# Six of seven layer-0 parts in high and low halves, a turn by 39 columns, and sum and halves placed sooner in a DLRM tower kernel

## The reference

```python
e = stack of the 39 gathered rows                        # (512, 39, 16)
x0 = xk = e
for W in (f0, f1, f2):                                   # (39*39, 128), (128*39, 128), (128*39, 128)
    z = einsum('bfd,bgd->bfgd', x0, xk).reshape(b, f * g, d)
    xk = einsum('bpd,pm->bmd', z, W)
    outs.append(xk)
h = concat(sum(concat(outs, 1), -1), dense_ctx)          # (512, 384 + 16)
y = relu(relu(h @ W1 + b1) @ W2 + b2) @ W3
```

## Time and profile before

| | |
|---|---|
| runs | 699.26 us median of 3 (698.6 to 702.59) |
| profiled execution | 700.51 us, span of its instructions 698.7 us |
| granted TensorE clock | 0.985 over the span, 1.00 in the loop |
| busy | PE 643.2, DVE 538.7, ACT 518.5, POOL 429.9 us |

### The profile page before, as it was taken

The page is one execution under the profiler, slowest core; times in us unless marked ns, Lnnn a source line. Parts: engine busy times, 40 slices in busy tenths (PEclk is TensorE's granted clock), DMA queues, the critical chain, the costliest instruction groups (busy, mean ns, idle before and its releaser), DMA issues. The chain is left out here.

```text
span 698.7 us, 11739 instructions
## 1 busy us (share of the span) xinstructions
PE 643.2 (92%) x2567; PEld 472.3 (68%) x2567; DVE 538.7 (77%) x1216; ACT 518.5 (74%) x1842; POOL 429.9 (62%) x416
## 2 busy tenths in 40 slices
PE   0578999999999999999999999999999999999988
PEld 0246777676767677777777676767676777776663
DVE  1426788888887979797988888888979797999880
ACT  1226688788797878787887888787878787888862
POOL 6876568686767676767678686767676534101330
PEclk9877999999999999999999999999999999999999
DMA  7551332231304040313131221313040320301000
GB/s 206 117 118 30 88 74 45 45 72 37 80 10 106 9 107 3 85 31 77 39 77 40 56 61 39 77 23 93 9 108 4 96 63 0 109 0 44 29 1 0
DMA packets 58221, 40.28 MB, mean 58 GB/s; under 512 B 36626, under 2 KB 41056, under 8 KB 58203
## 3 DMA queue, kind: packets, MB, share of 16 engines
q1 hardware_dynamic: 52376, 38.73, 22.1%
q0 software_dynamic: 5120, 1.29, 2.4%
q10 hardware_dynamic: 706, 0.06, 0.1%
HBM read 38.13 MB, written 1.94 MB: 57 GB/s over the span
## 5 line engine op out<-in xcount | busy, mean ns | idle before, releaser
L640 ACT ACTIVATE parts<-psa,x0c 128x128 f32<-128x128 f32 x1536 | 440.7, 431 | 94.6 <-PE psa L793 88.2
L532 DVE SCALAR_TENSOR_TENSOR parts<-psd,x0c,parts 128x128 f32<-128x128 f32 x960 | 266.0, 342 | 80.9 <-PE psd L793 64.1
L503 DVE TENSOR_REDUCE cur<-parts 128x64 f32<-128x1536 f32 x128 | 223.6, 1747 | 23.7 <-ACT parts L640 18.8
L789 PE MATMUL psa<-w1h,x1h 128*128 128x512 f32 x384 | 175.3, 457 | 5.9 <-issue 5.9
L793 PE MATMUL psa<-w1h,x1l 128*128 128x512 f32 x384 | 152.4, 397 | 0.0
L790 PE MATMUL psa<-w1l,x1h 128*128 128x512 f32 x384 | 152.2, 396 | 0.0
L359 POOL TENSOR_TENSOR z0l<-pairs,z0h 117x512 fp32r<-117x512 f32 x56 | 72.7, 1298 | 122.6 <-ACT z0h L596 122.4
L343 POOL DMA_INDIRECT emb<-tables,idx x130 | 126.7, 975 | 23.3 <-issue 19.8
L352 POOL TENSOR_TENSOR pairs<-x0t,pairs 117x512 f32<-117x512 f32 (+1 forms) x105 | 135.1, 1296 | 7.3 <-DMA x0t<-x_rows 6.6
L789 PE MATMUL psd<-w1h,x1h 128*128 128x512 f32 (+1 forms) x256 | 115.2, 450 | 12.1 <-DVE parts L532 12.1
L793 PE MATMUL psd<-w1h,x1l 128*128 128x512 f32 (+1 forms) x256 | 97.8, 382 | 0.0
(11 more groups left out here) (83 smaller groups left out, 524.5 us busy)
## 6 DMA issues: line engine op xcount, KB each, us to landing
pairs<-x_rows SPq DMA_DIRECT2D x113, 156.0 KB
pairs<-x_rows SPq DMA_DIRECT2D x30, 234.0 KB
x0t<-x_rows SPq DMA_DIRECT2D x16, 234.0 KB
emb<-tables,idx POOLq DMA_INDIRECT x130
x_rows<-emb SPq DMA_DIRECT2D x13, 72.0 KB
wt_sb<-w_top SPq DMA_DIRECT2D x1, 768.0 KB, 5.9
parts<-w SPq DMA_DIRECT2D x1, 704.0 KB, 4.9
x_rows<-emb SPq DMA_DIRECT2D x13, 40.0 KB
```

The source lines that it names most:

```text
L503: return dve.tensor_reduce(cur1[:, t % 2, first:end], terms[:, first:end, :, :], AX.XY, ALU.add)
L532: op = dve.scalar_tensor_tensor(acc, y[:, M * j:M * j + M], x0c[:, t, GF * g + j:GF * g + j + 1], acc, ALU.mult, ALU.add)
L640: op = act.activation(lanes(dst, j), y[:, M * j:M * j + M], ACT.Copy, scale=x0c[:, t, GF * g + j:GF * g + j + 1])
L789: pe.matmul(y[:, 0:n], hi, w1h[:, c], start=True, stop=False)
```

## The change

- `SPLIT` has parts 0 to 5; part 6 stays plain and is now the last one. The halves lie in rings, five buffers for high and four for low ones, so a sixth high half waits for part 0 of the same block, the fifth and sixth low half for parts 0 and 1.
- The three early halves of block b + 2 are made behind ACT (2,4), (3,2) and (3,4) (before: part 2 alone, at (3,4)); POOL subtracts 0 and 1 ahead of its last gather, 2 behind it.
- Parts 0, 1 and 2 of layer 0 go one group sooner, part 6 from (1,5) to (1,9), the turn from (0,8) to (0,9).
- The turn is a plain matmul of 39 rows and 39 columns instead of a transpose of 117.
- Sum over d: DVE (2,2) to (2,0). High halves of x1: ACT (2,4), (3,0), (3,2) to (2,1), (2,3), (3,0). Low halves: DVE (2,3), (3,0), (3,1) to (2,1), (2,2), (3,1). Block 0 keeps its own places for these.

```diff
-L0_AT = {(0, 5): 0, (0, 7): 1, (0, 9): 2, (1, 1): 3, (1, 3): 4, (1, 5): 6, (1, 8): 5}
-L0_AT_FIRST = {(1, 6): 0, (1, 8): 1, (2, 0): 2, (2, 2): 3, (2, 4): 4, (2, 6): 6, (2, 8): 5}
-TURN_AT, TURN_AT_FIRST = (0, 8), (1, 5)
+L0_AT = {(0, 4): [0], (0, 6): [1], (0, 8): [2], (1, 1): [3], (1, 3): [4], (1, 8): [5], (1, 9): [6]}
+L0_AT_FIRST = {(1, 6): [0], (1, 8): [1], (2, 0): [2], (2, 2): [3], (2, 4): [4], (2, 6): [5], (2, 8): [6]}
+TURN_AT, TURN_AT_FIRST = (0, 9), (1, 5)
-SPLIT = [2, 3, 4, 5]
-L0_END = 5
+SPLIT = [0, 1, 2, 3, 4, 5]
+L0_END = 6
+HIGHS, LOWS = 5, 4
-ZH_EARLY_AT = {(3, 4): 2}
+ZH_EARLY_AT = {(2, 4): 0, (3, 2): 1, (3, 4): 2}
-SUM_AT, SUM_AT_FIRST = (2, 2), (3, 0)
-HIGH_AT = {(2, 4): 0, (3, 0): 1, (3, 2): 2}
+SUM_AT, SUM_AT_FIRST = (2, 0), (3, 0)
+HIGH_AT = {(2, 1): 0, (2, 3): 1, (3, 0): 2}
-LOW_AT = {(2, 3): 0, (3, 0): 1, (3, 1): 2}
+LOW_AT = {(2, 1): 0, (2, 2): 1, (3, 1): 2}
...
+        def high_slot(i):
+            return z0h[0:ROWS, COLS * (i % HIGHS):COLS * (i % HIGHS) + COLS]
+
+        def low_slot(i):
+            return z0l[0:ROWS, COLS * (i % LOWS):COLS * (i % LOWS) + COLS]
...
                 pool.wait_ge(z0h_ready, (b - 2) * NS + i + 1)
+                pool.wait_ge(l0_steps, L0T * b + (SPLIT[i - LOWS] + 1 if i >= LOWS else 0))
...
                 if gather_ahead:
                     gather(8)
                 if ahead2:
+                    pair_low_part(b + 2, 0)
+                    pair_low_part(b + 2, 1)
+                if gather_ahead:
+                    gather(9)
+                if ahead2:
                     pair_low_part(b + 2, 2)
-                if gather_ahead:
-                    gather(9)
...
                 act.wait_ge(z0_ready, (b - 1) * L0T + k + 1)
-                act.wait_ge(l0_steps, L0T * b)
+                act.wait_ge(l0_steps, L0T * b + (SPLIT[i - HIGHS] + 1 if i >= HIGHS else 0))
...
-                act.activation(x0c[:, t, 0:F], pst[:, ROWS * t:ROWS * t + F], ACT.Copy).then_inc(x0c_ready, 1)
+                act.activation(x0c[:, t, 0:F], pst[:, F * t:F * t + F], ACT.Copy).then_inc(x0c_ready, 1)
...
-                    op = pe.transpose(pst[:, ROWS * t:ROWS * t + ROWS], x0t[0:ROWS, 128 * t:128 * t + 128], ident_sb[0:ROWS, :])
+                    op = pe.matmul(pst[:, F * t:F * t + F], x0t[0:F, 128 * t:128 * t + 128], ident_sb[0:F, :], start=True, stop=True)
```

More of the change, by code:

```diff
@@ L137, in build @@
         mask_sb = sb("mask_sb", [128, TB])
-        ident_sb = sb("ident_sb", [128, ROWS])
+        ident_sb = sb("ident_sb", [128, F])
         ids_sb = sb("ids_sb", [128, (NBLK + 1) * CH], I32)
@@ L148, in build @@
         pairs = sb("pairs", [128, L0T, COLS])
-        z0h = sb("z0h", [128, NS * COLS], F32R)
-        z0l = sb("z0l", [128, NS * COLS], F32R)
+        z0h = sb("z0h", [128, HIGHS * COLS], F32R)
+        z0l = sb("z0l", [128, LOWS * COLS], F32R)
         x1h = sb("x1h", [128, COLS], F32R)
@@ L357, in pair_low_part @@
                 pool.wait_ge(z0h_ready, (b - 2) * NS + i + 1)
-                c = slice(COLS * i, COLS * i + COLS)
-                pool.tensor_tensor(z0l[0:ROWS, c], pairs[0:ROWS, k, :], z0h[0:ROWS, c].bitcast(F32),
+                pool.wait_ge(l0_steps, L0T * b + (SPLIT[i - LOWS] + 1 if i >= LOWS else 0))
+                pool.tensor_tensor(low_slot(i), pairs[0:ROWS, k, :], high_slot(i).bitcast(F32),
                                    ALU.subtract).then_inc(z0l_ready, 1)
@@ L390, in first_block @@
                 gather_early(0, 9)
+                pair_low_part(2, 0)
+                pair_low_part(2, 1)
                 pair_low_part(2, 2)
@@ L438, in block_of @@
                 if ahead2:
-                    pair_low_part(b + 2, 2)
+                    pair_low_part(b + 2, 0)
+                    pair_low_part(b + 2, 1)
                 if gather_ahead:
                     gather(9)
+                if ahead2:
+                    pair_low_part(b + 2, 2)
             pool.wait_ge(ids_in, 16)
@@ L593, in pair_high_part @@
                 act.wait_ge(z0_ready, (b - 1) * L0T + k + 1)
-                act.wait_ge(l0_steps, L0T * b)
-                c = slice(COLS * i, COLS * i + COLS)
-                act.activation(z0h[0:ROWS, c], pairs[0:ROWS, k, :], ACT.Copy).then_inc(z0h_ready, 1)
+                act.wait_ge(l0_steps, L0T * b + (SPLIT[i - HIGHS] + 1 if i >= HIGHS else 0))
+                act.activation(high_slot(i), pairs[0:ROWS, k, :], ACT.Copy).then_inc(z0h_ready, 1)
             def high_part(b, t):
@@ L660, in block_of @@
                                 scalars(b + 1, SCALARS_AT[t, n])
-            act.dma_start(ident_sb[0:ROWS, :], ident).then_inc(const_in, 16)
+            act.dma_start(ident_sb[0:F, :], ident).then_inc(const_in, 16)
             act.dma_start(mask_sb[:, :], mask).then_inc(const_in, 16)
@@ L739, in layer0 @@
                     pe.wait_ge(z0l_ready, (b - 2) * NS + i + 1)
-                    c = slice(COLS * i, COLS * i + COLS)
                     w = slice(M * i, M * i + M)
-                    pe.matmul(ps0[:, :], w0h[0:ROWS, w], z0h[0:ROWS, c], start=False, stop=False)
-                    pe.matmul(ps0[:, :], w0h[0:ROWS, w], z0l[0:ROWS, c], start=False, stop=False)
-                    pe.matmul(ps0[:, :], w0l[0:ROWS, w], z0h[0:ROWS, c], start=False, stop=(k == L0_END)).then_inc(l0_steps, 1)
+                    pe.matmul(ps0[:, :], w0h[0:ROWS, w], high_slot(i), start=(k == 0), stop=False)
+                    pe.matmul(ps0[:, :], w0h[0:ROWS, w], low_slot(i), start=False, stop=False)
+                    pe.matmul(ps0[:, :], w0l[0:ROWS, w], high_slot(i), start=False, stop=(k == L0_END)).then_inc(l0_steps, 1)
                     return
@@ L795, in block_of @@
                             l0_at = L0_AT_FIRST if starts(b) else L0_AT
-                            if (t, g) in l0_at:
-                                layer0(b + 1, l0_at[t, g])
+                            for k in l0_at.get((t, g), []):
+                                layer0(b + 1, k)
                             if (t, g) == (TURN_AT_FIRST if starts(b) else TURN_AT):
@@ L809, in _ @@
             turn_x0(0)
-            for k in [*(k for k in range(L0T) if k != L0_END), L0_END]:
+            for k in range(L0T):
                 layer0(0, k)
@@ L918 @@
         "sample_mask": samples.astype(np.float32),
-        "identity": np.eye(ROWS, dtype=np.float32),
+        "identity": np.eye(F, dtype=np.float32),
     }
```

## The result

The changed kernel takes 735.14 us (median of 4, 734.08 to 736.92) against 700.64; the ratio is 1.050, with a 95% interval of 1.048 to 1.052. The forecast, slower, was right in direction. In size it was not: +14 us were forecast, +34.5 came, above the range.

The account below looks back on a forecast made before the run. TensorE was taken to bound the kernel (busy 432.3 of 447.4 us). Halves -0.31, turn +0.44, order +0.85 gave +0.98 a block, +12.7 over thirteen, +14.2 in all: 714.7, or 713.5 us by the median; range 702 to 719.

Parts of the forecast that it names:

- The new wait of ACT behind (2,1): In tile 2 ACT, behind its product and the gram copy, waits 1.43 us for the sum over d.
- the stall on psa at g8: In tile 2 TensorE waits for a psa buffer that ACT frees late: 0.94 us a block, where it had none.
- the wait of part 0 moved to g4: Layer 0, tile 0: TensorE waits for DVE's last low half, 0.57 us a block (was 0.70).
- a turn that costs more: The turn as eight matmul instructions, each exposing a 0.107 us weight load: 0.86 us, +0.44 a block.
- The stalls at g6 and g9 of tile 3: TensorE's stalls at these two groups: 0.75 us (was 0.54) and 0.60 us (was 0.78).
- But its first product of tile 2 needs g1, which ends at 334.70: DVE 334.90: DVE's first product of tile 2 waits for its TensorE group, starts at 334.90 and ends at 335.93.
- The halves: Two more parts of layer 0 in halves: TensorE -0.31 us a block in 14 blocks, POOL's cost nothing.
- ACT's copies: Two more copies on ACT at 0.52 us each, 1.04 us a block, counted in the chain.
- Cheap turns (1): Rival: turns as cheap as their columns, each 0.59 us less, 15 times -8.8: 704.6 us; chance 0.18.
- The ACT wait soaked up (2): Rival: ACT's new wait is absorbed, stalls stay at 2.01 us a block: 702.4 us; chance 0.11.
- Loads of 0.189 (4): Rival: the turn's weight loads run one after another at full length, +9.9 us: 723 us; chance 0.05.
- Faster (3): Rival: sooner halves free the block's end, stalls fall to about 0.6 us: 684 us; chance 0.10.

Follow-up runs that it names:

- 117-row run: The kernel before with the turn alone changed to a plain matmul of 117 rows and 39 columns; ratio 1.0092, +6.4 us.
- b_plain39: The kernel before with the turn alone changed to a plain matmul of 39 rows and 39 columns; ratio 1.0134, +9.3 us.

## Why the prediction was right and wrong

**The direction** and the mechanism held. The new wait of ACT behind (2,1), the stall on psa at g8, the wait of part 0 moved to g4 and a turn that costs more all stand in the trace. The sooner sum took the stall at g8 away, the old turn gave its 0.79 us back, the later part 0 cut its wait to 0.41, and each time the time came down. The stalls at g6 and g9 of tile 3 were worked out as 0.75 and 0.60 and measured 0.74 and 0.61.

**The size** failed in three terms of the sum, all too small: the stall at g8 by 0.76 us a block, the turn by 0.35, the stall at part 0 by 0.49. With the reload (0.11) and the faster matmuls (-0.38) that is the 1.33 by which the block of 37.28 + 0.98 = 38.26 was missed.

- "But its first product of tile 2 needs g1, which ends at 334.70: DVE 334.90": this is the step that failed most. The product also needs ACT's first one of the tile. On the prediction's clock g0 runs from 333.30, and measured it is 352.51 - 350.34 = 2.17 us behind g0's start, so 335.47, 0.57 later. With 0.86 instead of 0.76 from the sum's start to ACT's copy (356.07 - 355.21) and g8 due 0.1 sooner, the stall is 1.70 and not 0.94.
- The turn: 0.107 us for each of eight loads was right (0.110). That the first load would hide behind the matmul before it did not hold with 39 rows: +0.31 us a block, which the 117-row run takes away.
- The stall at part 0: 1.06 instead of 0.57. DVE's low half starts 332.29 - 328.47 = 3.82 us into the tile instead of 3.57, since cur's first half, which waits for ACT's last product of tile 3, starts 1.11 us into it (329.58) instead of 0.87; and from its start to the part's first matmul it takes 0.70 us, not the 0.50 of the plain part. That the longer list of semaphores of a part in halves does this is argued from the code and was not tried by itself; the same 0.71 in the kernel with the halves alone fits it.

**The halves** were priced well on TensorE (-0.31) and on POOL (nothing). ACT's copies, 1.04 us, were charged to the chain; the run with the halves alone shows that in the old order they are free.

**The rivals.** Cheap turns (1): refuted by b_plain39. The ACT wait soaked up (2): refuted. Loads of 0.189 (4): refuted, the pitch is 0.11. Faster (3): not in this kernel, but the early sum was the right deciding point: put behind (1,3), it is done before that time, and in the kernel before, where nothing else was changed, the time falls by 2.2%.

## What to carry to other kernels

When a step is placed sooner, look up every wait of the instruction that then starts the chain, in the code and not only in the trace: a wait that earlier work covers has no row at its place, and it is uncovered by just such a move. Look also for rows of the same wait at other places; here tile 1 had one. Put a step that others wait for where its own engine would sit idle anyway, if its data are there by then; here one place was worth 3.7% of the time. Fewer rows and columns do not make a small TensorE step cheap: count its weight loads, and look whether its neighbours use as many rows. And compare the pace of the untouched instructions too, before a difference between two blocks is put down to waits.

## What was not expected of the hardware

- A turn by plain matmuls of 39 rows costs 0.31 us more than one of 117 rows with the same columns, at its two borders.
- Eight exposed loads of 128 float32 columns follow each other at 0.110 us, though each lasts 0.189.
- In the changed kernel the three-matmul groups run at 0.229 to 0.230 us a matmul instead of 0.233, at the same granted clock of 1.00. The kernels with the new turn alone (0.2332), with the halves alone (0.2339) and with the order alone (0.2333) do not do so. Only kernels with all of the changed kernel's turn, halves and buffers do; no run here tells why.
